# Second layer norm of a fused recurrence and expert block: VectorE reads the two replicated statistics from PSUM, block by block

## The chip, the cores and the metric

One Trainium2 chip, all 8 cores. Each core computes one of the 8 sequences by itself; the cores exchange nothing. The metric is the device time of one execution, in microseconds, of the slowest core. A core has TensorE (PE in the profile), VectorE (DVE), ScalarE (ACT), GpSimd (POOL) and the queues that issue transfers (SP, and GpSimd's own).

## The reference

The input x has 8 sequences of 2048 tokens with 1024 channels, in f32. One layer is computed:

```python
x = x + attn(layernorm(x))      # both layer norms over channels, eps 1e-5
x = x + ffn(layernorm(x))

def attn(x, w_qkva, gamma):     # w_qkva [3072, 1024]
    h = rmsnorm(x) * gamma
    q, kv, a = split(h @ w_qkva.T, 3)
    a = sigmoid(a)
    # y[t] = a[t] * y[t-1] + kv[t], along the tokens
    return q * y

def ffn(x, W1, b1, W2, b2, Wg, bg):          # 8 experts, hidden size 128
    gate = softmax(x @ Wg + bg)
    h = relu(einsum('bsd,edh->bseh', x, W1) + b1)
    y = einsum('bseh,eho->bseo', h, W2) + b2
    return einsum('bse,bseo->bso', gate, y)
```

## The kernel before

Channels lie on the partitions and tokens run along the free dimension: x is handed over transposed and cut into 8 blocks (k, or d) of 128 channels. The 2048 tokens are worked in four chunks (c = 0 to 3) of TC = 512. A tile such as `x2_sb` or `hbf` is 128 x 8 x 512, one block per k. All weights stay in SBUF as bf16.

Per chunk the work goes through these functions, in this order:

- `emitB`: for each of 8 blocks the kv, a and q matmuls (lines 427, 446, 495; eight matmuls each), the sigmoid on ScalarE (458), the scan along the tokens on VectorE (469), the product with q on VectorE (506, into `y_sb`), and the residual addition on GpSimd (518, into `x2_sb` or `x2_sb2`, which the chunks take in turn, the function `x2buf`).
- `emitC`: ScalarE casts x2 to bf16 (533) and squares it (555), TensorE sums both over channels (545, 563), and VectorE and ScalarE make one row of means and one of reciprocal deviations (`emit_rows`, lines 218 to 242).
- `emitY2grp`, `emitOuts`: the previous chunk's second expert matmul, for output blocks d two at a time (853, 856; nine matmuls per block) and the addition into x2 on VectorE (870). It is strewn in between the current chunk's steps.
- `emitLoadXbf`, `emitS1`: the next chunk's x is loaded as bf16 by GpSimd's queue (268) and summed on TensorE (288).
- `emitRep2`: TensorE replicates the two rows over 128 partitions into `ps_rep` (579, 581; reciprocal deviation in bank 0, mean in bank 1), and VectorE copies both to `asig` in SBUF (589, 590).
- `emitLn2` (LN2): hbf = (x2 - mean) * rstd. VectorE does blocks 0 to 4, GpSimd blocks 5 to 7 (628, 631). VectorE takes blocks 0-1 and 2-3 in pairs of 128x1024 (604, 609) and block 4 alone (613, 617). Both engines read the statistics from `asig`.
- `emitScores`: eight matmuls of the gate (654). Block k waits for LN2's block k; in chunks 1 to 3 the first also waits for output addition 2. Then exp (662), its sum (672) and reciprocal (683).
- `emitE1`: the first expert matmul per expert (751), relu (811), replication of the gate into `ps_rep` (769, 801), the product into `h1g` (782, 832), and the next chunk's statistics (GpSimd's square at 315, sums at 331, rows, `emitRep1`). `emitPairs2` forms the next chunk's normed input (394).

The order on each engine is written out by hand; what an engine waits for are counts of one semaphore per engine. Each engine takes its instructions in order. `run_schedule` sets the order around the change. On VectorE it is: copies to `asig`, LN2's blocks, output additions 2, 3, 4, 5 of the previous chunk, the reciprocal of the gate's sum, additions 6 and 7. On TensorE: replication into `ps_rep`, the previous chunk's output groups 2, 3, 4 and 5, the scores, the sum, groups 6 and 7, the h1 matmuls. On GpSimd: residual additions, the issue of the xbf load, LN2's blocks 5 to 7, the square for the next chunk. `ps_rep` is written again by the gate's replication, which waits for VectorE's `g_bf` (705), behind LN2 in VectorE's order.

The copies that stay in both versions:

```python
vector.wait_ge(s_mm.h, K["mm_rep2"])
vector.tensor_copy(asig[:, 0, :], ps_rep[:, 0, :])
ii = vector.tensor_copy(asig[:, 1, :], ps_rep[:, 1, :])
s_dve.inc(ii)
```

Of the kernel before, what the change touches and what calls it, by code (L numbers as in the profile page):

```python
# [7 lines left out]
ALU = mybir.AluOpType  # L8
# [19 lines left out]
def build_program(T=2048, TC=512):  # L28
# [23 lines left out]
    with stack:  # L52
# [20 lines left out]
        hbf = sb("hbf", [128, KC, TC], BF16)  # L73
        y_sb = sb("y_sb", [128, KC, TC], F32)
        x2_sb = sb("x2_sb", [128, KC, TC], F32)
        x2_sb2 = sb("x2_sb2", [128, KC, TC], F32)
        asig = sb("asig", [128, 2, TC], F32)
# [8 lines left out]
        def x2buf(c):  # L86
            return x2_sb if c % 2 == 0 else x2_sb2
# [11 lines left out]
        ps_rep = ps("ps_rep", [128, 2, TC])  # L99
# [10 lines left out]
        s_dve = Sem(stack, nc, "s_dve")  # L110
# [17 lines left out]
        def on(eng, fn):  # L128
            state["on"](eng, fn)
# [5 lines left out]
        def rec_i(lst, i, sem):  # L135
            if state["counting"]:
                lst[i] = sem.n

        def init(d, key):
            if state["counting"]:  # L140
                d[key] = [0] * KC
# [453 lines left out]
        def emitLn2(c):  # L595
            K = ck[c]
            init(K, "ln2k")
            NDVE = 5
            for k0 in (0, 2, 4):
                def _ln2(vector, k0=k0):  # L600
                    if k0 == 0:
                        vector.wait_ge(s_dve.h, K["dve_evac"])
                    if k0 < 4:
                        s_dve.inc(vector.tensor_tensor(  # L604
                            y_sb[:, k0:k0 + 2, :], x2buf(c)[:, k0:k0 + 2, :],
                            asig[:, 1:2, :].to_broadcast([128, 2, TC]),
                            ALU.subtract))
                        vector.wait_ge(s_dve.h, s_dve.n)
                        ii = vector.tensor_tensor(  # L609
                            hbf[:, k0:k0 + 2, :], y_sb[:, k0:k0 + 2, :],  # L610
                            asig[:, 0:1, :].to_broadcast([128, 2, TC]), ALU.mult)
                    else:
                        s_dve.inc(vector.tensor_tensor(y_sb[:, k0, :],
                                                       x2buf(c)[:, k0, :],
                                                       asig[:, 1, :], ALU.subtract))
                        vector.wait_ge(s_dve.h, s_dve.n)
                        ii = vector.tensor_tensor(hbf[:, k0, :], y_sb[:, k0, :],
                                                  asig[:, 0, :], ALU.mult)
                    s_dve.inc(ii)
                on("vector", _ln2)  # L620
                rec_i(K["ln2k"], k0, s_dve)
                if k0 < 4:
                    rec_i(K["ln2k"], k0 + 1, s_dve)
            for k in range(NDVE, KC):
                def _ln2g(gpsimd, k=k):
                    if k == NDVE:
                        gpsimd.wait_ge(s_dve.h, K["dve_evac"])
                    s_gp.inc(gpsimd.tensor_tensor(y_sb[:, k, :], x2buf(c)[:, k, :],  # L628
                                                  asig[:, 1, :], ALU.subtract))
                    gpsimd.wait_ge(s_gp.h, s_gp.n)  # L630
                    ii = gpsimd.tensor_tensor(hbf[:, k, :], y_sb[:, k, :],  # L631
                                              asig[:, 0, :], ALU.mult)
                    s_gp.inc(ii)
                on("gpsimd", _ln2g)
                rec_i(K["ln2k"], k, s_gp)
            if state["counting"]:
                K["dve_ln2"] = K["ln2k"][NDVE - 1]
                K["gp_ln2"] = K["ln2k"][KC - 1]
            K["n_dve_ln2"] = NDVE
# [247 lines left out]
        def run_schedule():  # L887
# [23 lines left out]
            for c in range(NCH):  # L911
# [11 lines left out]
                if c > 0:  # L923
                    emitY2grp(c - 1, [2, 3], c)
                emitLn2(c)
                if c > 0:
                    emitOuts(c - 1, [2, 3])
# [106 lines left out]
```

## Time and profile before

| | us |
|---|---|
| median of 2 runs | 538.6 (538.58 to 538.61) |
| the profiled execution | 538.28 |
| its span on the slowest core (core 3) | 536.7 |
| spans of the 8 cores | 524.1 to 536.7 |
| TensorE busy | 413.1 (77%) |
| VectorE busy | 253.1 (47%) |
| GpSimd busy | 119.2 (22%) |
| ScalarE busy | 114.0 (21%) |

The span runs from the first to the last instruction; the execution's time has 1.6 us around it. The rows are those of core 3 unless they say otherwise. In a timeline a row gives the start, the duration, the engine, the line of the kernel, the operation, output and inputs with partitions x elements and type, and how many instructions were merged (x8); the bracket says how long the engine had been idle before and what released it. PE is TensorE's matmul, DVE VectorE, ACT ScalarE, POOL GpSimd.

### The profile page before, as it was taken

How to read it: one execution, taken by the hardware profiler on the slowest of the kernel's cores; microseconds unless marked ns; L12 is line 12 of the kernel's file. 1: busy time of each engine (PE TensorE's matmuls, PEld its weight loads, DVE VectorE, ACT ScalarE, POOL GpSimd, SP SyncE). 2: the span in 40 equal slices, each digit the busy share in tenths (PEclk: the TensorE clock that was granted, in tenths of full speed). 3: DMA queues.
4: the chain of work that ended last, by engine and by line, in shares of the span. 5: the costliest groups of instructions: out<-in, count | busy, mean ns of one | idle time of the engine just before them, and what ended most of it. 6: DMA issues, size and time to landing. Idle time of an engine off the chain costs nothing.

```text
span 536.7 us, 4715 instructions; the slowest of 8 cores (524.1 to 536.7 us)
## 1 busy us (share of the span) xinstructions
PE 413.1 (77%) x1540; PEld 151.4 (28%) x1540; DVE 253.1 (47%) x319; ACT 114.0 (21%) x179; POOL 119.2 (22%) x76
## 2 busy tenths in 40 slices
PE   1345599713779999767889998687989997858994
PEld 0101144200223444212323443122224442313231
DVE  0463434337465344528365434576554343873221
ACT  2120010720123112510222104500251026102200
POOL 5000012306700013119300024067000212430000
PEclk9955799966597999968978999998879999968888
DMA  7999992280000000720400000900400000004004
GB/s 120 222 169 157 165 166 41 70 167 0 0 0 2 0 1 1 184 52 0 158 0 1 1 0 1 234 2 0 156 1 0 1 0 1 1 0 158 0 0 156
DMA packets 18230, 32.05 MB, mean 60 GB/s; under 512 B 656, under 2 KB 4752, under 8 KB 18208
## 3 DMA queue, kind: packets, MB, share of 16 engines
q0 software_dynamic: 9584, 14.98, 18.0%
q1 hardware_dynamic: 8624, 16.79, 9.5%
q8 instruction: 13, 0.21, 0.2%
q14 instruction: 9, 0.07, 0.0%
HBM read 38.35 MB, written 8.39 MB: 87 GB/s over the span
## 4 chain that ended last, share of the span: by engine, by line
PE 56%; DVE 17%; DMA 16%; issue 4%; ACT 2%; another core or an unknown queue 2%; POOL 1%; DVEq 0%; ACTq 0%; POOLq 0%
PE ps_kv L427 10%; PE ps_a L446 10%; PE ps_q L495 9%; DMA xbf<-xT 9%; DMA wq_bf<-wqT 8%; PE ps_kv L751 7%; PE ps_a L856 4%; DVE hbf L609 3%; PE ps_a L751 3%; DVE y_sb L604 3%; DVE rows L235 2%; PE ps_a L654 2%; PE ps_kv L856 2%; PE ps_q L288 2%
## 5 line engine op out<-in xcount | busy, mean ns | idle before, releaser
L518 POOL TENSOR_TENSOR x_sb<-x_sb,y_sb 128x512 f32<-128x512 f32 x32 | 40.4, 1264 | 274.1 <-DVE y_sb L506 274.0
L427 PE MATMUL ps_kv<-hbf,wq_bf 128*128 128x512 bf16 x256 | 67.3, 397 | 16.4 <-DVE hbf L903 7.5
L446 PE MATMUL ps_a<-hbf,wq_bf 128*128 128x512 bf16 x256 | 62.7, 389 | 6.1 <-DVE wq_bf L199 6.1
L469 DVE TENSOR_TENSOR_SCAN y_sb<-asig,carry,ps_kv 128x512 f32<-128x512 f32 x24 | 30.7, 1280 | 63.5 <-ACT asig L458 63.5
L495 PE MATMUL ps_q<-hbf,wq_bf 128*128 128x512 bf16 x256 | 59.3, 379 | 0.1
L458 ACT ACTIVATE asig<-ps_a 128x512 f32<-128x512 f32 x32 | 19.1, 597 | 158.3 <-PE ps_a L446 158.3
L751 PE MATMUL ps_kv<-hbf,w_bf 128*128 128x512 bf16 x192 | 50.8, 421 | 0.0
L628 POOL TENSOR_TENSOR y_sb<-x_sb,asig 128x512 f32<-128x512 f32 x12 | 25.0, 2082 | 78.7 <-DVE asig L590 78.7
L427 PEld LDWEIGHTS ps_kv<-hbf,wq_bf 128*128 128x128 bf16 x256 | 25.6, 100 | 54.1 <-issue 29.0
L288 PE MATMUL ps_q<-xbf,statc 128*1 128x512 bf16 x32 | 12.4, 550 | 34.2 <-DMA xbf<-xT 34.2
L446 PEld LDWEIGHTS ps_a<-hbf,wq_bf 128*128 128x128 bf16 x256 | 25.5, 100 | 37.9 <-issue 9.5
L495 PEld LDWEIGHTS ps_q<-hbf,wq_bf 128*128 128x128 bf16 x256 | 25.0, 98 | 30.5 <-issue 1.0
L856 PE MATMUL ps_a<-h1g,w_bf 128*128 128x512 bf16 x128 | 33.5, 409 | 0.0
L654 PE MATMUL ps_a<-hbf,wg_bf 128*128 128x512 bf16 x32 | 14.2, 609 | 24.3 <-DVE x_sb L870 13.5
L856 PE MATMUL ps_kv<-h1g,w_bf 128*128 128x512 bf16 x128 | 31.8, 393 | 0.0
L832 DVE TENSOR_TENSOR h1g<-y_sb,ps_rep 128x512 bf16<-128x512 f32 x24 | 16.2, 686 | 29.1 <-ACT y_sb L811 23.1
L751 PEld LDWEIGHTS ps_kv<-hbf,w_bf 128*128 128x128 bf16 x192 | 19.3, 106 | 28.3 <-issue 12.0
L235 DVE RECIPROCAL rows<-rows 1x512 f32<-1x512 f32 x8 | 26.7, 3341 | 0.8
L811 ACT ACTIVATE y_sb<-ps_kv,b1s 128x512 f32<-128x512 f32 x24 | 16.0, 678 | 48.0 <-PE ps_kv L751 48.0
L506 DVE TENSOR_TENSOR y_sb<-ps_q,y_sb 128x512 f32<-128x512 f32 x32 | 22.1, 692 | 7.3 <-PE ps_q L495 6.4
L631 POOL TENSOR_TENSOR hbf<-y_sb,asig 128x512 bf16<-128x512 f32 x12 | 22.6, 1884 | 1.7
L218 DVE COPY rows<-ps_q 1x512 f32<-1x512 f32 x8 | 5.4, 676 | 34.1 <-PE ps_q L288 17.6
(85 smaller groups left out, 430.5 us busy)
## 6 DMA issues: line engine op xcount, KB each, us to landing
x_sb<-xT SPq DMA_DIRECT2D x4, 2048.0 KB, 13.9
outT<-x_sb SPq DMA_DIRECT2D x4, 2048.0 KB, 6.6
wq_bf<-wqT POOLq DMA_DIRECT2D x3, 2048.0 KB, 41.1
xbf<-xT POOLq DMA_DIRECT2D x3, 1024.0 KB, 16.5
w_bf<-w1p POOLq DMA_DIRECT2D x1, 2048.0 KB, 64.5
w_bf<-w2p POOLq DMA_DIRECT2D x1, 2048.0 KB, 76.5
xbf<-xT POOLq DMA_DIRECT2D x2, 512.0 KB, 11.5
wg_bf<-wgp POOLq DMA_DIRECT2D x1, 256.0 KB, 76.0
```

Of the source, the lines that this page charges most:

```text
L235: ii = vector.reciprocal(row(R_INV), row(R_S2))
L288: ii = tensor.matmul(ps_q[0:1, 0, :], statc[:], xbf[:, k, :], start=(k == 0), stop=(k == KC - 1))
L427: ii = tensor.matmul(ps_kv[:, j % 2, :], wq_bf[:, k, (8 + j) * 128:(9 + j) * 128], hbf[:, k, :], start=(k == 0), stop=(k == KC - 1))
L446: ii = tensor.matmul(ps_a[:, j % 2, :], wq_bf[:, k, (16 + j) * 128:(17 + j) * 128], hbf[:, k, :], start=(k == 0), stop=(k == KC - 1))
L469: s_dve.inc(vector.tensor_tensor_scan(y_sb[:, j, :], asig[:, j % 2, :], ps_kv[:, j % 2, :], init, ALU.mult, ALU.add))
L495: ii = tensor.matmul(ps_q[:, j % 2, :], wq_bf[:, k, j * 128:(j + 1) * 128], hbf[:, k, :], start=(k == 0), stop=(k == KC - 1))
L518: ii = gpsimd.tensor_tensor(x2buf(c)[:, j, :], x_sb[:, j, :], y_sb[:, j, :], ALU.add)
L628: s_gp.inc(gpsimd.tensor_tensor(y_sb[:, k, :], x2buf(c)[:, k, :], asig[:, 1, :], ALU.subtract))
L631: ii = gpsimd.tensor_tensor(hbf[:, k, :], y_sb[:, k, :], asig[:, 0, :], ALU.mult)
L654: ii = tensor.matmul(ps_a[:, 0, :], wg_bf[:, k, :], hbf[:, k, :], start=(k == 0), stop=(k == KC - 1))
L751: ii = tensor.matmul(pb[:, BM[e] % 2, :], w1_bf[:, k, e * 128:(e + 1) * 128], hbf[:, k, :], start=(k == 0), stop=(k == KC - 1))
L856: ii = tensor.matmul(pb[:, d % 2, :], w2_bf[:, e, d * 128:(d + 1) * 128], h1g[:, e, :], start=False, stop=(e == E - 1))
```

## The change

In LN2, VectorE's five blocks are taken one at a time in place of two pairs and one, so that ten instructions of 128x512 stand for four of 128x1024 and two of 128x512. Their second operand is the replicated mean or reciprocal deviation in `ps_rep` (PSUM, f32) in place of `asig` (SBUF, f32). VectorE's wait for its own copies to `asig` goes; the wait of each multiplication for its subtraction stays. The copies stay, and GpSimd's blocks 5 to 7 read `asig` as before. Each block has now its own count to wait for (blocks 0 and 1 had one in common, as had 2 and 3).

```diff
--- before.py
+++ after.py
@@ -596,31 +596,16 @@
             K = ck[c]
             init(K, "ln2k")
             NDVE = 5
-            for k0 in (0, 2, 4):
-                def _ln2(vector, k0=k0):
-                    if k0 == 0:
-                        vector.wait_ge(s_dve.h, K["dve_evac"])
-                    if k0 < 4:
-                        s_dve.inc(vector.tensor_tensor(
-                            y_sb[:, k0:k0 + 2, :], x2buf(c)[:, k0:k0 + 2, :],
-                            asig[:, 1:2, :].to_broadcast([128, 2, TC]),
-                            ALU.subtract))
-                        vector.wait_ge(s_dve.h, s_dve.n)
-                        ii = vector.tensor_tensor(
-                            hbf[:, k0:k0 + 2, :], y_sb[:, k0:k0 + 2, :],
-                            asig[:, 0:1, :].to_broadcast([128, 2, TC]), ALU.mult)
-                    else:
-                        s_dve.inc(vector.tensor_tensor(y_sb[:, k0, :],
-                                                       x2buf(c)[:, k0, :],
-                                                       asig[:, 1, :], ALU.subtract))
-                        vector.wait_ge(s_dve.h, s_dve.n)
-                        ii = vector.tensor_tensor(hbf[:, k0, :], y_sb[:, k0, :],
-                                                  asig[:, 0, :], ALU.mult)
+            for k in range(NDVE):
+                def _ln2(vector, k=k):
+                    s_dve.inc(vector.tensor_tensor(y_sb[:, k, :], x2buf(c)[:, k, :],
+                                                   ps_rep[:, 1, :], ALU.subtract))
+                    vector.wait_ge(s_dve.h, s_dve.n)
+                    ii = vector.tensor_tensor(hbf[:, k, :], y_sb[:, k, :],
+                                              ps_rep[:, 0, :], ALU.mult)
                     s_dve.inc(ii)
                 on("vector", _ln2)
-                rec_i(K["ln2k"], k0, s_dve)
-                if k0 < 4:
-                    rec_i(K["ln2k"], k0 + 1, s_dve)
+                rec_i(K["ln2k"], k, s_dve)
             for k in range(NDVE, KC):
                 def _ln2g(gpsimd, k=k):
                     if k == NDVE:
```

## Rows read from the trace of the kernel before

**Rows 1.** Page, the chain that ended last, share of the span by engine

```profile
...
PE 56%; DVE 17%; DMA 16%; issue 4%; ACT 2%; another core or an unknown queue 2%; POOL 1%; DVEq 0%; ACTq 0%; POOLq 0%
...
```

**Rows 2.** The chain in order of time, chunk 0: start us, us, what

```profile
...
135.00 1.57 DVE hbf L617
136.71 1.88 PE ps_a L654 x4
140.08 8.22 PE ps_kv L751 x24
...
```

**Rows 3.** Timeline, VectorE and GpSimd, LN2 of chunk 0: start us, us, engine

```profile
...
125.39 1.23 DVE L604 TENSOR_TENSOR y_sb<-x_sb,asig 128x1024 f32<-128x1024 f32 x1
125.44 2.29 POOL L628 TENSOR_TENSOR y_sb<-x_sb,asig 128x512 f32<-128x512 f32 x1 [22.34 <-DVE asig L590]
126.72 2.10 DVE L609 TENSOR_TENSOR hbf<-y_sb,asig 128x1024 bf16<-128x1024 f32 x1
127.88 2.06 POOL L631 TENSOR_TENSOR hbf<-y_sb,asig 128x512 bf16<-128x512 f32 x1
128.74 2.28 DVE L604 TENSOR_TENSOR y_sb<-x_sb,asig 128x1024 f32<-128x1024 f32 x1
...
135.00 1.56 DVE L617 TENSOR_TENSOR hbf<-y_sb,asig 128x512 bf16<-128x512 f32 x1
136.16 1.53 POOL L631 TENSOR_TENSOR hbf<-y_sb,asig 128x512 bf16<-128x512 f32 x1
...
```

**Rows 4.** Groups by form, whole run: busy us, mean ns

```profile
...
L518 POOL TENSOR_TENSOR x_sb<-x_sb,y_sb 128x512 f32<-128x512 f32 x32 | 40.4, 1264 | 274.1 <-DVE y_sb L506 274.0
...
L832 DVE TENSOR_TENSOR h1g<-y_sb,ps_rep 128x512 bf16<-128x512 f32 x24 | 16.2, 686 | 29.1 <-ACT y_sb L811 23.1 <-PE ps_kv L751 5.7 <-PE ps_rep L801 0.2
...
L222 DVE TENSOR_TENSOR rows<-rows 1x512 f32<-1x512 f32 x8 | 5.4, 671 | 0.0
...
```

**Rows 5.** Timeline, a GpSimd pair beside VectorE with a PSUM input, chunk 0

```profile
...
97.86 2.60 POOL L518 TENSOR_TENSOR x_sb<-x_sb,y_sb 128x512 f32<-128x512 f32 x2 [3.92 <-DVE y_sb L506]
98.36 0.69 DVE L506 TENSOR_TENSOR y_sb<-ps_q,y_sb 128x512 f32<-128x512 f32 x1 [0.64 <-PE ps_q L495]
...
```

**Rows 6.** Timeline, chunk 1: LN2's start, TensorE up to the h1 matmuls

```profile
...
239.90 1.23 DVE L604 TENSOR_TENSOR y_sb<-x_sb,asig 128x1024 f32<-128x1024 f32 x1
...
246.57 1.90 PE L856 MATMUL ps_kv<-h1g,w_bf 128*128 128x512 bf16 x8
...
251.94 3.49 PE L654 MATMUL ps_a<-hbf,wg_bf 128*128 128x512 bf16 x8 [3.46 <-DVE x_sb L870]
...
260.86 5.34 PE L751 MATMUL ps_kv<-hbf,w_bf 128*128 128x512 bf16 x24
...
```

**Rows 7.** Timeline, chunk 2: LN2's start, scores, h1 matmuls

```profile
...
353.12 1.23 DVE L604 TENSOR_TENSOR y_sb<-x_sb,asig 128x1024 f32<-128x1024 f32 x1
...
365.15 3.21 PE L654 MATMUL ps_a<-hbf,wg_bf 128*128 128x512 bf16 x8 [5.04 <-DVE x_sb L870]
...
373.79 5.34 PE L751 MATMUL ps_kv<-hbf,w_bf 128*128 128x512 bf16 x24
...
```

**Rows 8.** Timeline, chunk 3: the same, and the group behind the scores

```profile
...
462.73 1.23 DVE L604 TENSOR_TENSOR y_sb<-x_sb,asig 128x1024 f32<-128x1024 f32 x1
...
474.76 3.57 PE L654 MATMUL ps_a<-hbf,wg_bf 128*128 128x512 bf16 x8 [5.04 <-DVE x_sb L870]
...
480.30 3.59 PE L856 MATMUL ps_a<-h1g,w_bf 128*128 128x512 bf16 x8
...
485.90 5.34 PE L751 MATMUL ps_kv<-hbf,w_bf 128*128 128x512 bf16 x24
...
```

**Rows 9.** Granted clock of chunk 3's scores; core 0's chunk 1, scores and h1

```profile
...
474.76:478.34 3.58, 3.57 (x8) 1.07 (x8) 1.54 (x3) 0.00 (x0) 0.27 (x1) 0.50 0.00 0
...
250.97 1.89 PE L654 MATMUL ps_a<-hbf,wg_bf 128*128 128x512 bf16 x8 [2.37 <-DVE x_sb L870]
...
258.29 4.05 PE L751 MATMUL ps_kv<-hbf,w_bf 128*128 128x512 bf16 x18
...
```

## The prediction

> **What bounds the kernel now.** I read the page's chain of waits by engine first [rows 1]. TensorE's work makes up 56% of the chain that ended last, VectorE's 17%. So most of the time is not where this change works, and the question is in which stretches VectorE or GpSimd decides. The chain in order of time answers it. Its rows here [rows 2] are, for chunk 0, VectorE's last multiplication, the score matmuls and the h1 matmuls; in each of the four chunks the second layer norm (I call it LN2) is on the chain, from the first subtraction to the moment when the score matmuls may run, and it is VectorE's instructions that stand there, one behind the other.
>
> The third view is the timeline of that stretch with VectorE and GpSimd side by side [rows 3]. The first subtraction, 128x1024 f32, takes 1.23 us. The same instruction, issued again at 128.74, takes 2.28. The last multiplication, a single block of 128x512, takes 1.56, more than the first one took for twice the elements. So the length isn't set by the elements. Look at the ends instead: VectorE 126.62, GpSimd 127.73, VectorE 128.82, GpSimd 129.94, VectorE 131.02: they alternate. Each engine finishes about 1.1 us after the other has finished, though both were issued long before. These two engines take turns at something. In these rows all have both inputs in SBUF (x2 and y_sb with asig). The whole stretch is a sum of turns: VectorE runs from 125.39 to 136.56 (11.2 us), GpSimd from 125.44 to 137.69 (12.25 us). The pattern repeats in all four chunks with the same durations.
>
> Does an instruction of VectorE with one input in PSUM take part in this? One place shows it [rows 5]: two GpSimd additions at 97.86 take 2.60 us together, 1.30 each, while VectorE multiplies ps_q by y_sb at 98.36 in 0.69 us. Over the whole run GpSimd's addition takes 1264 ns on average and VectorE's 128x512 multiplication with a PSUM input 686 ns [rows 4]. A turn would have made VectorE's 0.69 longer by up to 1.1 us; it isn't. So a PSUM operand seems to keep VectorE out of the turns.
>
> **The change on VectorE.** Six instructions go (four of 128x1024, two of 128x512); ten of 128x512 come, each with x2 or y_sb in SBUF and ps_rep in PSUM. The nearest rows are the h1g multiplication (SBUF f32 by PSUM f32, bf16 out, 686 ns) [rows 4] and the multiplication by ps_q (f32 out, 0.69) [rows 5]: I take 0.69 each. The multiplication waits for its subtraction: it starts 0.10 us behind the end of that (125.39 + 1.23 = 126.62, start 126.72). The next subtraction waits for nothing and starts 0.08 before the end (126.72 + 2.10 = 128.82, start 128.74) [rows 3]. One block so costs 0.69 + 0.10 + 0.69 - 0.08 = 1.40, five cost 7.0 us, where 11.1 went before: 4.1 us less per chunk. The wait for the copies in front of the first subtraction goes too; since the copies are VectorE's own, the start moves from 0.10 behind them to 0.08 before their end, 0.18 us. The copies to asig themselves stay, since GpSimd reads them.
>
> The Trainium skill has a rule that speaks against this (VectorE: DVE Perf Modes, sections "Rules for kernel authors" and "The TRN2 errata"): for many operations on a matmul's output one copies it to SBUF first, and a PSUM source has a fixed cost of 120 cycles where an SBUF source has 58, at 0.96 GHz. As an estimate by that page the ten would cost 10 x 0.065 = 0.65 us more than from SBUF. In the trace the difference is smaller: 671 ns for a 512-element f32 multiplication out of SBUF beside 686 with PSUM [rows 4], 0.15 us over the ten. The page's price would take 0.65 us from each chunk where VectorE decides, and leave the sign.
>
> **The change on GpSimd**, whose code isn't touched. Its three blocks are two instructions each, 2.29 and 2.06 us, with turns of VectorE in them. Alone, the same shape in f32 takes 1.26 [rows 4]; the part of a turn behind VectorE's end is 1.12 (128.82 to 129.94) [rows 3]. I take 1.26 and keep 1.12 as the low bound, the 2.06 to 2.29 of now as the high one. With 0.15 between subtraction and multiplication: 3 x (1.26 + 0.15 + 1.26) = 8.0 in place of 12.25, 4.25 us less.
>
> **What that is worth, chunk by chunk.** The scores take blocks 0 to 4 from VectorE and 5 to 7 from GpSimd; in chunks 1 to 3 they also wait for output addition 2, queued on VectorE behind LN2, and stand on TensorE behind four groups of the previous chunk's second matmul.
> - Chunk 0 [rows 2, 3]: the last four score matmuls start at 136.71 and are done at 138.58. After: VectorE is through at 132.4, GpSimd at 125.44 + 8.0 = 133.44, and the last matmul ends about 0.8 later (0.14 to wake, 0.6 for one at the low clock), at 134.2. Gain 4.4. GpSimd is what is late now.
> - Chunk 1 [rows 6]: LN2 starts at 239.90, the scores at 251.94. VectorE would let them start at 239.90 + 7.0 + 0.94 = 247.8 (0.94 is from the start of the addition, 11.1 behind LN2's, to the scores), but TensorE has its groups to finish until 246.57 + 1.90 = 248.5. TensorE becomes the limit: gain 3.4.
> - Chunks 2 and 3 [rows 7, 8]: from LN2's start to the scores 12.03 us in both (353.12 to 365.15, 462.73 to 474.76). After: 7.0 + 0.94 - 0.18 = 7.8. Gain 4.25 each, and GpSimd (8.0, with its last block used only after seven matmuls) is in time.
>
> Sum 4.4 + 3.4 + 8.5 = 16.3 us. All of it lies on the chain, and the next chunk's load of xbf, its sums and its first matmuls start from there, so I cost nothing of it away.
>
> **TensorE's clock.** In chunks 1 to 3 TensorE stood still for 3.5 to 5.0 us in front of the scores (the brackets in [rows 6, 7, 8]), and the eight scores took 3.49, 3.21 and 3.57 us; the granted clock of the last of these stretches, the third figure from the end of its row, is 0.50, that is 1.2 GHz [rows 9]. In chunk 3 the group behind them was slow too, 3.59 for what takes 1.90 elsewhere. Core 0, whose pause in chunk 1 was 2.37 us, had the eight at 2.4 GHz in 1.89, and went from the scores to the h1 matmuls in 258.29 - 250.97 = 7.3 us [rows 9]. On core 3 that way took 8.9, 8.6 and 11.1 us [rows 6, 7, 8]. After the change the pause is 0 in chunk 1 and about 0.9 in the others, so I expect 7.3 everywhere: gains of 1.6, 1.3 and 3.8, together 6.7. This is the soft part of the sum. The bounds are 0 and, since any other group of nine may move by 1.7 us either way when the phases shift, some 5 us more.
>
> Forecast: 16.3 + 6.7 = 23.0 us off the profiled execution's 538.3 (its span and 1.6 around it), 515.3; the median of the runs is 0.3 above it: **515.5 us**.
>
> **Rivals.**
> A: the clock gives nothing back; the scores stay at 1.2 GHz because of the waits for exp and for the second statistics around them. Then 16.3 alone: 522.3. For it: in chunk 0 the 24 h1 matmuls behind the scores take 8.22 us [rows 2], in chunk 1 5.34 [rows 6], so the clock can stay low past the scores. Against: core 0.
> B: GpSimd doesn't speed up, its 2.0 to 2.3 us are its own. Then the last block comes 12.3 us behind the start of LN2 as now, and its matmul ends 0.55 later: gains 0.1 and, from the scores' ends of now (255.4, 368.4, 478.3) against 239.9, 353.1 and 462.7 plus 12.85, 2.7, 2.4 and 2.8. Together 8.0: 530.6. Against: 1.26 for the same shape [rows 4], and ends that follow VectorE's.
> C, the one on the slower side: the taking of turns persists, because y_sb and hbf are still written in SBUF and x2 read there. A turn of VectorE for 128x1024 costs 1.08 (129.94 to 131.02 [rows 3]), so one for 128x512 half of that, 0.54, and one of GpSimd 1.12. Six and six alternate, 10.0 us, and four more of VectorE take 2.8: 12.8 in place of 11.1, because more and smaller instructions each wait for a longer one. It is slower than now from a turn of 0.26 us upwards (6 x (0.26 + 1.12) + 2.8 = 11.1). 1.7 us more in each chunk: 545.3. Against: [rows 5]. The Trainium skill (SBUF — State Buffer, section "Who interferes with whom") says that VectorE needs two SBUF inputs for this, reading being what is shared; by that rule C can't happen.
> D: more clock than counted, the shorter pauses keeping further groups fast: three groups of nine at 1.7, 5 us more, 510.5. For it: 3.59 against 1.90 [rows 6, 8]. Against: the pauses behind the h1 matmuls, for the gate, stay as they are.
>
> **How the numbers follow.** Forecast 0.60, A 0.20, D 0.10, B 0.06, C 0.04. The range runs from 509 (D, with GpSimd's turns at their low bound of 1.12 in chunk 0, 0.8 us) to 525 (A with one or two groups of nine at 1.2 GHz more, 1.7 us each). A measurement of this kernel tells about 2% from no change, that is 527.8 and 549.4: forecast, A and D are faster (0.90, less 0.01 for what I haven't thought of), B and C lie within 2% (0.10), and slower by more gets 0.01.
>
> **What would show it.** VectorE's ten LN2 instructions at 0.62 to 0.69 us, whatever GpSimd does beside them; GpSimd's six at 1.26; the scores in chunk 1 directly behind TensorE's group, in 2 and 3 about 7.8 us behind the start of LN2; eight scores in 1.9 us. Instructions of VectorE above 1 us there would mean C; GpSimd still at 2 us, B; scores of 3.5 us, A. The forecast is wrong altogether if the gained time comes back as a longer wait for xbf's load, whose start only moves with the chain.

## The result and the profile after

The changed kernel takes 518.0 us (median), 0.960 of the kernel before (95% interval 0.957 to 0.963): 4.0% less, about 21.7 us of 538.9. The forecast was 515.5 us, with a range of 509 to 525. In some executions, of the kernel before as well, one die runs some per cent longer at a lower granted clock; all ratios leave these out.

The profiled execution took 516.0 us (538.3 before) and has a span of 514.4 us on core 7, where the one before had 536.7 on core 3. The mean span of the eight cores fell from 531.4 to 509.0. The chain that ended last, share of the span by engine, from the page:

```profile
...
PE 61%; DMA 17%; DVE 12%; issue 3%; ACT 2%; another core or an unknown queue 2%; POOL 1%; DVEq 0%; ACTq 0%; POOLq 0%
...
```

VectorE's share of the chain has gone from 17% to 12% [rows 1]. The timeline of LN2 in chunk 0, VectorE, GpSimd and TensorE (start us, us, engine, line; LN2's lines are now 601 and 604 on VectorE, 613 and 616 on GpSimd, the scores 639, the h1 matmuls 736):

```profile
...
126.04 0.68 DVE L601 TENSOR_TENSOR y_sb<-x_sb,ps_rep 128x512 f32<-128x512 f32 x1
126.28 1.26 POOL L613 TENSOR_TENSOR y_sb<-x_sb,asig 128x512 f32<-128x512 f32 x1 [22.38 <-DVE asig L590]
126.82 0.69 DVE L604 TENSOR_TENSOR hbf<-y_sb,ps_rep 128x512 bf16<-128x512 f32 x1
127.43 0.68 DVE L601 TENSOR_TENSOR y_sb<-x_sb,ps_rep 128x512 f32<-128x512 f32 x1
...
127.68 1.27 POOL L616 TENSOR_TENSOR hbf<-y_sb,asig 128x512 bf16<-128x512 f32 x1
...
132.96 1.26 POOL L616 TENSOR_TENSOR hbf<-y_sb,asig 128x512 bf16<-128x512 f32 x1
...
133.21 1.86 PE L639 MATMUL ps_a<-hbf,wg_bf 128*128 128x512 bf16 x4 [0.80 <-DVE hbf L604]
...
136.50 0.13 PEld L736 LDWEIGHTS ps_kv<-hbf,w_bf 128*128 128x128 bf16 x2 [0.47 <-issue]
...
```

Set this beside [rows 3]. VectorE's and GpSimd's instructions lie across each other and neither is longer for it: 0.68 and 0.69 beside 1.26 and 1.27. No end of the one follows the end of the other any more. VectorE starts at 126.04 and is through after 7.0 us, where it took 11.2; GpSimd ends at 134.22, 7.9 us after its start, where it took 12.25. The groups by form over the whole run say the same (busy us, mean ns):

```profile
...
L616 POOL TENSOR_TENSOR hbf<-y_sb,asig 128x512 bf16<-128x512 f32 x12 | 15.2, 1268 | 1.7
L613 POOL TENSOR_TENSOR y_sb<-x_sb,asig 128x512 f32<-128x512 f32 x12 | 15.2, 1268 | 82.1 <-DVE asig L590 82.1
...
L604 DVE TENSOR_TENSOR hbf<-y_sb,ps_rep 128x512 bf16<-128x512 f32 x20 | 13.7, 687 | 2.1
L601 DVE TENSOR_TENSOR y_sb<-x_sb,ps_rep 128x512 f32<-128x512 f32 x20 | 13.6, 679 | 0.0
...
```

Chunk 1, VectorE's first subtraction, TensorE's last group of the previous chunk, the output additions, the scores, the h1 matmuls. It answers to [rows 6]:

```profile
...
234.14 0.68 DVE L601 TENSOR_TENSOR y_sb<-x_sb,ps_rep 128x512 f32<-128x512 f32 x1
...
240.97 1.90 PE L841 MATMUL ps_kv<-h1g,w_bf 128*128 128x512 bf16 x8
...
241.09 1.28 DVE L855 TENSOR_TENSOR x_sb<-ps_a,x_sb 128x512 f32<-128x512 f32 x2
...
242.70 1.89 PE L639 MATMUL ps_a<-hbf,wg_bf 128*128 128x512 bf16 x8
...
250.02 5.34 PE L736 MATMUL ps_kv<-hbf,w_bf 128*128 128x512 bf16 x24
...
```

The row of the scores has no bracket: TensorE came from its group, which ends at 242.87, without a pause (matmuls are pipelined, so a row can start before the end of the one in front). VectorE would have let them start at 242.03 (output addition 2 starts at 241.09, and before it was 0.94 from there to the scores). So TensorE is what decides here, as the prediction had it. Chunk 2 is alike, which the prediction did not have: behind a late replication the first of the previous chunk's groups (L841) runs at the low clock.

```profile
...
343.60 3.59 PE L841 MATMUL ps_a<-h1g,w_bf 128*128 128x512 bf16 x8
...
344.55 0.68 DVE L601 TENSOR_TENSOR y_sb<-x_sb,ps_rep 128x512 f32<-128x512 f32 x1
...
354.12 1.89 PE L639 MATMUL ps_a<-hbf,wg_bf 128*128 128x512 bf16 x8
...
```

Chunk 3, beside [rows 8]:

```profile
...
449.88 0.68 DVE L601 TENSOR_TENSOR y_sb<-x_sb,ps_rep 128x512 f32<-128x512 f32 x1
...
457.75 1.89 PE L639 MATMUL ps_a<-hbf,wg_bf 128*128 128x512 bf16 x8 [0.69 <-DVE x_sb L855]
...
465.07 5.34 PE L736 MATMUL ps_kv<-hbf,w_bf 128*128 128x512 bf16 x24
...
```

From LN2's start to the scores 7.87 us (12.03 before), from the scores to the h1 matmuls 7.32 (11.14). The granted clock of these scores, the third figure from the end:

```profile
...
457.75:459.65 1.90, 1.89 (x8) 0.74 (x8) 1.54 (x3) 0.00 (x0) 0.32 (x1) 1.00 0.00 0
...
```

It was 0.50 in [rows 9]. The same two stretches, read from the timelines of all eight cores for chunks 1 to 3 (24 stretches a kernel):

| | LN2's start to scores, mean | pause before the scores | eight scores in 1.89 us | scores to h1 matmuls, mean |
|---|---|---|---|---|
| before | 12.04 | 2.1 to 5.0 | 7 of 24 | 9.47 |
| after | 8.58 (7.9 where VectorE decides) | 0 to 0.7 | 24 of 24 | 7.32 |

So per core the mean gain in three chunks is 3 x (12.04 - 8.58) = 10.4 us of position and 3 x (9.47 - 7.32) = 6.5 us of clock.

### The profile page after: what moved, and what is told of

It reads as the page before. It is cut to its first block, busy times and chain, and to the rows that moved or that the text cites. A ratio compares the mean times of both kernels' runs of the same rounds, so it can differ in the third digit from the quotient of the medians.

```text
span 514.4 us, 4735 instructions; the slowest of 8 cores (503.4 to 514.4 us)
## 1 busy us (share of the span) xinstructions
PE 405.8 (79%) x1540; PEld 149.8 (29%) x1540; DVE 235.3 (46%) x335; ACT 114.0 (22%) x179; POOL 102.0 (20%) x76
## 4 chain that ended last, share of the span: by engine, by line
PE 61%; DMA 17%; DVE 12%; issue 3%; ACT 2%; another core or an unknown queue 2%; POOL 1%; DVEq 0%; ACTq 0%; POOLq 0%
PE ps_kv L427 11%; PE ps_a L446 10%; PE ps_q L495 10%; DMA xbf<-xT 9%; DMA wq_bf<-wqT 8%; PE ps_kv L736 7%; PE ps_a L841 6%; PE ps_kv L841 3%; PE ps_a L736 3%; DVE rows L235 3%; PE ps_q L288 2%; PE ps_a L639 1%; DVE wq_bf L199 1%; DVE hbf L604 1%
## 5 line engine op out<-in xcount | busy, mean ns | idle before, releaser
L458 ACT ACTIVATE asig<-ps_a 128x512 f32<-128x512 f32 x32 | 19.1, 597 | 159.5 <-PE ps_a L446 159.5
L736 PE MATMUL ps_kv<-hbf,w_bf 128*128 128x512 bf16 x192 | 48.7, 407 | 0.0
L288 PE MATMUL ps_q<-xbf,statc 128*1 128x512 bf16 x32 | 13.9, 605 | 35.4 <-DMA xbf<-xT 35.4
L841 PE MATMUL ps_a<-h1g,w_bf 128*128 128x512 bf16 x128 | 33.8, 412 | 0.0
L841 PE MATMUL ps_kv<-h1g,w_bf 128*128 128x512 bf16 x128 | 31.8, 393 | 0.0
L613 POOL TENSOR_TENSOR y_sb<-x_sb,asig 128x512 f32<-128x512 f32 x12 | 15.2, 1268 | 82.1 <-DVE asig L590 82.1
L817 DVE TENSOR_TENSOR h1g<-y_sb,ps_rep 128x512 bf16<-128x512 f32 x24 | 16.2, 685 | 26.5 <-ACT y_sb L796 21.7
L315 POOL TENSOR_TENSOR tbf<-xbf 128x4096 bf16<-128x4096 bf16 x3 | 21.0, 7012 | 0.0
L211 ACT ACT_TABLE_LOAD x16 | 20.5, 1283 | 1.5 <-ACT y_sb L796 0.4
```

The lines of the kernel that those rows point to most:

```text
L211: ii = scalar.activation(plscr[:], plscr[:], func)
L288: ii = tensor.matmul(ps_q[0:1, 0, :], statc[:], xbf[:, k, :], start=(k == 0), stop=(k == KC - 1))
L315: ii = gpsimd.tensor_tensor(xsq[:], xbf[:], xbf[:], ALU.mult)
L736: ii = tensor.matmul(pb[:, BM[e] % 2, :], w1_bf[:, k, e * 128:(e + 1) * 128], hbf[:, k, :], start=(k == 0), stop=(k == KC - 1))
L841: ii = tensor.matmul(pb[:, d % 2, :], w2_bf[:, e, d * 128:(d + 1) * 128], h1g[:, e, :], start=False, stop=(e == E - 1))
```

## The experiments

Each kernel was timed beside the kernel before on the same chip; ratios are against that one.

**e1: small blocks, operands in SBUF.** The changed kernel, with asig for ps_rep:

```diff
+                    if k == 0:
+                        vector.wait_ge(s_dve.h, K["dve_evac"])
                     s_dve.inc(vector.tensor_tensor(y_sb[:, k, :], x2buf(c)[:, k, :],
-                                                   ps_rep[:, 1, :], ALU.subtract))
+                                                   asig[:, 1, :], ALU.subtract))
                     vector.wait_ge(s_dve.h, s_dve.n)
                     ii = vector.tensor_tensor(hbf[:, k, :], y_sb[:, k, :],
-                                              ps_rep[:, 0, :], ALU.mult)
+                                              asig[:, 0, :], ALU.mult)
```

> The ten small instructions of the changed kernel, but with both statistics read from asig in SBUF (and the wait for the copies kept). Theory (VectorE and GpSimd take turns while both instructions read two operands from SBUF; the operand's place made the gain): the turns persist, VectorE's LN2 takes 12.8 us per chunk where it took 11.1, the time is about 545 us, 1.2% above the kernel before. Rival R1 (a PSUM operand is quicker for VectorE by itself, GpSimd has no part): about as before, 539. Rival R2 (small blocks with counts of their own made the gain): as the changed kernel, 517.

568.4 us, ratio 1.054 (1.050 to 1.057). R2 has fallen: the small blocks alone make the kernel slower. It is slower than the theory said, too, by 23 us. Its timeline in chunk 0, a multiplication of VectorE (L606), the last of GpSimd's LN2 (L618), and GpSimd's square for the next chunk (L315):

```profile
...
134.61 1.56 DVE L606 TENSOR_TENSOR hbf<-y_sb,asig 128x512 bf16<-128x512 f32 x1
135.77 1.53 POOL L618 TENSOR_TENSOR hbf<-y_sb,asig 128x512 bf16<-128x512 f32 x1
...
137.26 7.46 POOL L315 TENSOR_TENSOR tbf<-xbf 128x4096 bf16<-128x4096 bf16 x1
137.95 7.31 DVE L606 TENSOR_TENSOR hbf<-y_sb,asig 128x512 bf16<-128x512 f32 x1
...
```

GpSimd has only six instructions in LN2, VectorE ten. When GpSimd has finished its six it doesn't fall silent: its queue holds the square of 128x4096, 7 us. Here the turn lasts as long as that whole instruction. VectorE's multiplication, issued at 137.95, ends at 145.26, 0.54 us after the square. From LN2's start to the scores it is therefore 20.4 us in chunks 1 and 2, and 13.8 in chunk 3, which has no square behind it. Chunk 1:

```profile
...
249.73 0.69 DVE L603 TENSOR_TENSOR y_sb<-x_sb,asig 128x512 f32<-128x512 f32 x1
...
270.12 3.57 PE L641 MATMUL ps_a<-hbf,wg_bf 128*128 128x512 bf16 x8 [11.69 <-DVE x_sb L857]
...
```

**e9: e1 with the square held back.**

```diff
                 gpsimd.wait_ge(s_mm.h, ck[c - 1]["mm_s2b"])
+                gpsimd.wait_ge(s_dve.h, ck[c - 1]["dve_ln2"])
                 ii = gpsimd.tensor_tensor(xsq[:], xbf[:], xbf[:], ALU.mult)
```

> e1 (ten small instructions from asig) with one wait more: GpSimd's square for the next chunk starts only when VectorE's LN2 is through. In e1's trace VectorE's fourth multiplication waits 7.3 us behind that square in chunks 0 to 2. If that one turn is what put e1 at 568 where rival C was priced at 545, LN2 to scores takes 13.8 us in all of chunks 1 to 3, as it did in e1's chunk 3, which has no square, and the time falls by 3 x 4.3 = 13 to some 20 us (with a shorter pause for TensorE's clock), to 545 to 555 us. If the small blocks had a cost of their own in SBUF, it stays above 560.

547.9 us, ratio 1.016 (1.006 to 1.027): inside what I had expected, and slower than the kernel before by 0.6 to 2.7%. Chunk 1 of its trace, GpSimd's last LN2 instruction (L619), VectorE's multiplications beside and behind it (L607), the square (L316) and the scores (L642):

```profile
...
250.42 1.57 DVE L607 TENSOR_TENSOR hbf<-y_sb,asig 128x512 bf16<-128x512 f32 x1
251.58 1.53 POOL L619 TENSOR_TENSOR hbf<-y_sb,asig 128x512 bf16<-128x512 f32 x1
...
253.75 0.69 DVE L607 TENSOR_TENSOR hbf<-y_sb,asig 128x512 bf16<-128x512 f32 x1
...
255.99 7.01 POOL L316 TENSOR_TENSOR tbf<-xbf 128x4096 bf16<-128x4096 bf16 x1 [2.89 <-DVE hbf L607]
...
256.70 3.57 PE L642 MATMUL ps_a<-hbf,wg_bf 128*128 128x512 bf16 x8 [5.07 <-DVE x_sb L858]
...
```

From 253.11 on GpSimd is silent, and the same VectorE instruction that took 1.57 beside it takes 0.69. LN2 to the scores is 13.8 us in all three chunks (256.70 - 242.93), on all cores. The one wait is worth 20 us: an added wait that makes a kernel faster. It saves 6.6 us in each of the three chunks with a square behind them: 20.4 to 13.8 in chunks 1 and 2, and 24.4 to 17.7 from the copies to the h1 matmuls in chunk 0, which my expectation had left out. What is left over the kernel before is the price of small turns against long ones, 13.8 against 12.0 us: on the mean of the cores 7.3 us from the copies to the h1 matmuls, of the 1.6% or 8.8 us.

**e2: pairs, operands in PSUM.** The kernel before, its two pairs kept:

```diff
                         s_dve.inc(vector.tensor_tensor(
                             y_sb[:, k0:k0 + 2, :], x2buf(c)[:, k0:k0 + 2, :],
-                            asig[:, 1:2, :].to_broadcast([128, 2, TC]),
+                            ps_rep[:, 1:2, :].to_broadcast([128, 2, TC]),
                             ALU.subtract))
```

and the same in the other three places, and without the wait for the copies.

> The kernel before with its two pairs and one single block, only the operand moved from asig to ps_rep. Theory: VectorE's pairs take 1.23 us each and LN2 2 x 2.48 + 1.40 = 6.4 us (7.0 in the changed kernel); GpSimd's six at 1.27. TensorE or GpSimd hides most of the 0.6 in chunks 0 to 2: 516.5 to 517.5 us. R1: the same. R2: no gain, 538.

514.6 us, ratio 0.956 (0.953 to 0.959), 1.9 us below the range that I had given. Timeline, chunk 0, pair subtraction and pair multiplication of VectorE, GpSimd between them:

```profile
...
125.92 1.21 DVE L602 TENSOR_TENSOR y_sb<-x_sb,ps_rep 128x1024 f32<-128x1024 f32 x1
126.16 1.26 POOL L626 TENSOR_TENSOR y_sb<-x_sb,asig 128x512 f32<-128x512 f32 x1 [23.80 <-DVE asig L590]
127.24 1.22 DVE L607 TENSOR_TENSOR hbf<-y_sb,ps_rep 128x1024 bf16<-128x1024 f32 x1
...
```

1.21 and 1.22 us for 1024 elements, where [rows 3] has 2.10 for the same multiplication. So the operand's place gives the whole gain (with the wait for the copies, 0.18 us a chunk, which goes along with it), and the split into single blocks none. The median is even 3.4 us below the changed kernel's, which was timed apart from it, but the intervals overlap (up to 0.959 here, from 0.957 there), so whether pairs are better isn't settled. The traces have LN2 to the scores at 7.24 us where VectorE decides, against 7.87.

**e5: all eight blocks on VectorE, operands in SBUF, GpSimd idle.** The kernel before with

```diff
-            NDVE = 5
-            for k0 in (0, 2, 4):
+            NDVE = 8
+            for k0 in (0, 2, 4, 6):
```

all of them pairs from asig, and the square held as in e9. The sigmoid, which writes into `asig`, waits for VectorE's last block in place of GpSimd's.

> The kernel before, with all eight LN2 blocks on VectorE in four pairs from asig, and GpSimd's square for the next chunk held until they are done, so that GpSimd is idle. Theory (turns): every instruction of 128x1024 takes 1.23 us although both operands lie in SBUF, LN2 takes 4 x 2.48 = 9.9 us for eight blocks where five took 11.1 with GpSimd's help. Scores 1.2 us earlier in chunks 1 to 3, 2.1 in chunk 0, and perhaps some of the clock: 530 to 534 us, faster than the kernel before with half the engines at work. R1 (VectorE is slow from SBUF by itself): 8 x 2.1 = 16.8 us, 5.7 later in each chunk, 561 us.

531.7 us, ratio 0.988 (0.983 to 0.993): a small gain, as expected and clear of the noise. Timeline, chunk 0, the first pair:

```profile
...
127.07 1.23 DVE L605 TENSOR_TENSOR y_sb<-x_sb,asig 128x1024 f32<-128x1024 f32 x1
128.40 1.23 DVE L610 TENSOR_TENSOR hbf<-y_sb,asig 128x1024 bf16<-128x1024 f32 x1
...
```

1.23 us each, and all of them, in every chunk and on every core, are 1.22 or 1.23. R1 has fallen: SBUF operands (1.23) are as quick as PSUM operands (1.22 in e2) as long as GpSimd is silent. In the kernel before, GpSimd's help was worth less than nothing: VectorE does eight blocks alone in 10.0 us and needed 11.2 for five with it.

**e3: only the subtractions read PSUM.**

```diff
                     ii = vector.tensor_tensor(hbf[:, k, :], y_sb[:, k, :],
-                                              ps_rep[:, 0, :], ALU.mult)
+                                              asig[:, 0, :], ALU.mult)
```

> As the changed kernel, but the multiplications read the reciprocal deviation from asig; the subtractions keep ps_rep. Theory: subtractions at 0.68 us beside GpSimd, multiplications at 0.69 to 1.8 (their own 0.54 and what is left of GpSimd's 1.12), VectorE's LN2 about 10 us, GpSimd's about 10.5 to 11: 530 to 536 us. R1: each PSUM operand is worth the same, half of the gain, 528, with all multiplications equally long. R2: 517.

524.8 us, ratio 0.976 (0.972 to 0.981): between, but better than I expected. Timeline, chunk 0, a subtraction of GpSimd (L613) with VectorE's subtraction from PSUM (L601) and multiplication from SBUF (L604) beside it:

```profile
...
129.03 1.71 POOL L613 TENSOR_TENSOR y_sb<-x_sb,asig 128x512 f32<-128x512 f32 x1
129.54 0.67 DVE L601 TENSOR_TENSOR y_sb<-x_sb,ps_rep 128x512 f32<-128x512 f32 x1
...
130.32 0.97 DVE L604 TENSOR_TENSOR hbf<-y_sb,asig 128x512 bf16<-128x512 f32 x1
...
```

VectorE's subtraction runs through at 0.67 inside GpSimd's turn; the multiplication issued behind it waits for what is left of that turn (it ends 0.55 behind GpSimd's end at 130.74) and takes 0.97. I had not counted that the free subtraction eats up most of the turn that the multiplication would otherwise wait for: VectorE's LN2 takes 8.75 us and not 10. R1 doesn't fit here either: the first multiplication of each chunk takes 1.27 and the four others 0.97, the same operands each time. LN2 to the scores is 9.6 us. The turns belong to the single instruction and its operands, not to the stage.

**e4: the pause given back.** The changed kernel with work for nothing behind VectorE's LN2 in chunks 1 to 3:

```diff
+            if c > 0:
+                def _fill(vector):
+                    vector.wait_ge(s_dve.h, s_dve.n)
+                    s_dve.inc(vector.tensor_copy(row(R_T0), row(R_S2)))
+                    vector.wait_ge(s_dve.h, s_dve.n)
+                    s_dve.inc(vector.reciprocal(row(R_GI), row(R_T0)))
+                on("vector", _fill)
```

> The changed kernel with work that isn't needed behind VectorE's LN2 in chunks 1 to 3: a copy and a reciprocal of one row of 512, some 3.9 us, in front of output addition 2. It gives TensorE back its pause before the scores and leaves both LN2 halves free of turns. By position alone: the filler less the slack that the additions have in the changed kernel's profile (0.7 in chunk 1, 1.7 in chunk 2, none in chunk 3), 3.2 + 2.2 + 3.9 = 9.3 us, 527 us. If the pause also costs TensorE its clock in the scores and the group behind, as in the kernel before, up to 6.7 us more: 533 us, eight scores at 3.5 us instead of 1.9.

537.3 us, ratio 0.998 (0.996 to 0.999): the gain is gone, and 4 us more than expected with it. Some 3 of these 4 us are position: the filler is 4.7 us long (241.99 in chunk 1 to 246.69, where the next addition starts), not 3.9. Timeline, chunk 1, GpSimd's last LN2 instruction (L623), the copy (L612), the reciprocal (L614):

```profile
...
241.78 1.27 POOL L623 TENSOR_TENSOR hbf<-y_sb,asig 128x512 bf16<-128x512 f32 x1
...
241.99 1.34 DVE L612 COPY rows<-rows 1x512 f32<-1x512 f32 x1
...
243.43 3.34 DVE L614 RECIPROCAL rows<-rows 1x512 f32<-1x512 f32 x1
...
```

The copy has one input, in SBUF, and takes 1.34 us; a one-row operation of 512 elements, the cast in line 221, takes 0.42 when GpSimd is still (a copy of such a row with GpSimd still is in no trace). All 24 copies stand beside GpSimd's last instruction and take 1.33 to 1.35. The one shown ends 0.28 us behind GpSimd's instruction (243.05). So one SBUF input is enough for a copy to take its turn, which I hadn't expected from [rows 5]. The Trainium skill says it (SBUF — State Buffer, section "Who interferes with whom"): a copy can run in a mode that uses both ports and then contends, whereas a `tensor_tensor` contends by its second SBUF input. As to who waits the trace agrees, with 1.34 for the copy, and with 0.68 beside GpSimd for a `tensor_tensor` with one SBUF input.

LN2's start to the scores is 12.7 us, 4.1 more than after the change on average over the 24 stretches, 12.4 us in three chunks where I had 9.3. The clock comes back as I had priced it. The scores to the h1 matmuls are back at a mean of 9.55 us where the changed kernel has 7.32 everywhere: 6.7 us in three chunks. Together 19.1 of the some 20 us between the two kernels by their ratios (0.998 and 0.960). Granted clock in chunk 3, scores and the group behind them (the third figure from the end):

```profile
...
473.82:477.40 3.58, 3.57 (x8) 1.07 (x8) 1.54 (x3) 0.00 (x0) 0.00 (x0) 0.50 0.00 0
479.36:482.90 3.54, 3.54 (x10) 1.08 (x9) 2.99 (x1) 0.00 (x0) 0.00 (x0) 0.53 0.00 0
...
```

Nothing about these matmuls was changed; what is new is that TensorE had stood still for 5.52 us in front of them. Of the 24 stretches, those with a pause of 2.5 to 2.9 us had the scores in 1.89, and every one above 3.8 had at least some of them at the low clock. The length of the pause doesn't decide alone, though. In the chunks 1 to 3 of all eleven traces together, the scores took 1.89 us behind every pause up to 1.3 us and behind none above 3.4; of the 30 pauses between 2.1 and 3.0 us, 19 left them at 1.89 and 11 did not (9 of these in e3, 2.33 to 2.77 us behind pauses of 2.42).

**e6, e7, e8: where the gained time would come back.** The prediction named a longer wait for xbf's load as what would undo it. The load is issued from GpSimd's queue behind the residual additions, though its buffer is free before `emitB` begins. Moved there in the changed kernel (e6), in the kernel before (e7), in e2 (e8):

```diff
             for c in range(NCH):
+                if c + 1 < NCH:
+                    emitLoadXbf(c + 1)
                 emitB(c)
...
                 if c + 1 < NCH:
-                    emitLoadXbf(c + 1)
                     emitS1(c + 1)
```

> The changed kernel with the next chunk's load of xbf issued ahead of emitB in place of behind it. TensorE's waits for that load (10.2, 5.6 and some 2.6 us in the changed kernel's trace) should go; the replication then waits for the row of deviations, 14.6 us behind the last product with q as in chunk 3, in place of 22.5, 22.3 and 17.9, plus up to 3 us for the sums of xbf in front: 10 to 16 us less, 501 to 507 us. Rival: the load collides with the weights' and with x_sb's and comes no earlier in chunk 0: 5 to 8 us less.

489.9 us, ratio 0.910 (0.904 to 0.916), 11 us below the range that I had given.

> The kernel before with the same earlier load. If LN2's gain and the load's are independent stretches of the chain, the two differ by as much as the kernels with the late load (4%): 523 to 529 us. If the change's gain depended on the load's wait in any way, the distance to e6 is smaller than 21 us.

521.3 us, ratio 0.968 (0.962 to 0.973), 2 us below my range.

> Pairs from PSUM and the earlier load: VectorE's LN2 6.4 us in place of 7.0; since TensorE binds in chunks 1 and 2, 0 to 1 us below e6.

490.6 us in the profiled execution, ratio 0.912 (0.906 to 0.918), e6's within the intervals. My reason, that TensorE hides what the pairs save, doesn't hold: LN2 to the scores is 7.5 us on average where e6 has 7.9, and TensorE itself is late in 3 of the 24 stretches only. The mean span of the cores is all the same 486.3 against 486.2. Where the saved half microsecond a chunk goes is not shown.

The waits for that load on the slowest core of the changed kernel (us in total, times, longest):

```profile
...
PE ps_q L288 <- DMA xbf<-xT: 35.4, 5, 10.4
...
```

and in e6:

```profile
...
PE ps_q L288 <- DMA xbf<-xT: 15.4, 2, 10.4
...
```

20 us of it are gone; what is left are the two halves of the first chunk's load, at the start. The sums of xbf (L288) in front of chunk 1's LN2, in the changed kernel (core 7):

```profile
...
226.83 3.57 PE L288 MATMUL ps_q<-xbf,statc 128*1 128x512 bf16 x8 [5.61 <-DMA xbf<-xT]
...
```

The same sums in e6, with the replication (L579), LN2's start and the scores:

```profile
...
212.48 1.89 PE L288 MATMUL ps_q<-xbf,statc 128*1 128x512 bf16 x8
...
214.30 1.12 PE L579 MATMUL ps_rep<-rows,ones_f 1*128 1x512 f32 x2
...
216.94 0.68 DVE L601 TENSOR_TENSOR y_sb<-x_sb,ps_rep 128x512 f32<-128x512 f32 x1
...
224.83 1.89 PE L639 MATMUL ps_a<-hbf,wg_bf 128*128 128x512 bf16 x8 [0.70 <-DVE x_sb L855]
...
```

The sums now run at a granted clock of 1.00 in 1.89 us directly before the replication, where they took 3.57 at 0.50 behind a wait, and LN2 starts at 216.9 in place of 234.1. I had e6 at 501 to 507 and was wrong by more than 10. From the start to the first LN2, and from each LN2 to the next, it gains 8.3, 8.9, 7.9 and 1.5 us (126.0 to 117.7; 108.1 to 99.2; 110.4 to 102.6; 105.3 to 103.9). From the start of the last product with q to the replication, core 7 of the changed kernel has 22.5, 22.3 and 20.0 us in chunks 0 to 2, and e6 has 14.5, 14.9 and 14.9, sums and all: 20.5 us. I had 17.9 for the third, which isn't core 7's, and added up to 3 us for the sums, which cost next to nothing. Another 2.2 us are scores that no longer stand behind TensorE in chunks 1 and 2. Where the last 4 lie wasn't worked out. The cores now end within 4.8 us of each other (483.1 to 487.9), where they spread over 11.0 (503.4 to 514.4).

The distance between e7 and e6 is 31.4 us, where the late load had 21.7. I had put down a smaller distance as the sign that the gain depends on the load's wait; it does depend, and the distance is larger. In e7 the pause before the scores is 5.0 to 5.2 us on all cores in chunks 1 and 2, and the way from the scores to the h1 matmuls has a mean of 10.9 us; in e6 the pause is 0.7 to 0.9 and the way 7.3. Position 3 x 4.15, the earlier start 3 x 0.19 and clock 3 x 3.54, with chunk 0's 4.3, are 28.0 of the 31.4; with the late load the same steps give 21.8. Of the 6 us between, 2 are position: with the early load TensorE no longer reaches the replication late and at the low clock, and VectorE decides in all 24 stretches of e6. The other 4 are clock: the pause of e7 costs more than that of the kernel before (on average 4.7 us long against 3.8, and 10.9 us from the scores to the h1 matmuls against 9.5), so there is more to give back.

## Why the prediction was right

By its own steps, on the slowest core of each profile:

| step | forecast | measured |
|---|---|---|
| VectorE's LN2 | 7.0 us, 0.69 each | 7.0, 0.68 and 0.69 |
| start against the copies | 0.18 earlier | 0.19 (125.45 + 0.68 - 126.04 = 0.09 before their end, 0.10 behind it before) |
| GpSimd's LN2 | 8.0 us, 1.26 each | 7.9, 1.27 |
| chunk 0, copies to h1 matmuls | 4.4 less | 4.4 (16.0 to 11.7) |
| chunk 1: position, clock | 3.4, 1.6 | 3.7, 1.6 |
| chunk 2: position, clock | 4.25, 1.3 | 2.65, 1.3 |
| chunk 3: position, clock | 4.25, 3.8 | 4.35, 3.8 |

Position is the way from LN2's start to the scores, with the 0.19 of the earlier start; clock is the way from there to the h1 matmuls. The sum comes to 21.8 us where I had 23.0. By its span the profiled execution gained 22.3 us. The difference between 23.0 and 21.8 has one place: in chunk 2 of core 7 TensorE reached the replication behind a late load, ran the previous chunk's first group at the low clock (3.59 us) and was not through with its four groups when VectorE was; VectorE took 7.0 us but the scores started after 9.57. I had read that limit in chunk 1 of core 3 and taken chunk 2 as VectorE's. On the eight cores, TensorE decides in 11 of the 24 stretches.

The table sets core 3 of one trace against core 7 of another, and how well single lines agree is in part luck. From LN2 to LN2 and on to the end, core 7 is shorter than core 3 by 6.4, 2.8, 4.3 and 9.5 us, where the steps say 4.4, 5.3, 4.0 and 8.2; the ways between the stages moved by up to 2.5 us either way and cancelled. The firmer ground is the mean of all eight cores: the same steps give 4.3 + 10.4 + 0.6 + 6.5 = 21.8 us, and the spans 22.3. So almost nothing came back elsewhere, as the prediction had assumed; the waits for xbf's load in front of the three later chunks are 18.0 us a core before and 17.8 after. The profiled execution is 0.7 us above its forecast of 515.3. The median is 2.5 us above the forecast of 515.5, since the profiled execution is one of the quicker ones: those that the ratio counts run from 514.4 to 522.0, a spread wider than the step from the forecast to rival A.

The core of the argument was that VectorE and GpSimd take turns, and that a PSUM operand frees VectorE. Both are shown: the first by e5 (GpSimd silent, SBUF operands, 1.23 us) and e9 (the same instruction at 1.57 and then 0.69), the second by e2 and e3. In e3 the two kinds stand one behind the other. That it is the reading of the second operand, and not the writing, rests on these kernels writing the same tiles in SBUF with and without turns.

The clock was the soft part and the 6.7 us were right, by the means of 24 stretches (6.5) and by e4 (6.7 back). Rival A (no clock) would have been 522.3. The time alone, 518.0, lies between it and the forecast and doesn't exclude it; the 24 scores of 1.89 us do. D asked for 5 us more and didn't come: the previous chunk's groups of eight matmuls lose 4.8 us to the low clock on core 7, where core 3 lost 4.4 before.

Rival B fell with GpSimd's 1.27. Rival C did not occur, and e9 is the kernel in which it does: I had priced it at 545.3 us and 1.7 us a chunk; measured are 547.9 us and 1.74 a chunk (13.78 - 12.04). But that price held only with the square held back. Where the turns really persisted (e1), the price was 568. The step that failed there is "four more of VectorE take 2.8": I asked what VectorE does when GpSimd has finished its share of LN2, and not what GpSimd does next. For the chance of C it made no difference; had C come, it would have been outside my range and slower by more than 2%, not within it. The price of a PSUM operand did not show: subtraction and multiplication take 679 and 687 ns with it here, 685 and 693 ns from SBUF beside a silent GpSimd in e9. (The 671 ns that I had set beside the 686 were of an instruction on one partition.) By the Trainium skill (VectorE: DVE Perf Modes, section "The TRN2 errata", 120 cycles against 58) it would have been, as an estimate, 0.65 us a chunk; the measurement decides.

## What to carry to other kernels

When two engines' instructions end one behind the other at a fixed distance although both were issued long before, they take turns, and the first question is which operand puts them there; moving one operand to PSUM freed both engines here. Price such a turn by the longest instruction that can stand in the other engine's queue, also the one behind the stage, and check whether dividing or delaying the work is better before adding help. Where a stage in front of TensorE gets shorter, add what the pause cost TensorE's clock, which here was two fifths of the gain from position, and look for the next late thing: here a load issued behind work that it doesn't need, worth some 27 us more by the ratios.

## What I had not expected

- A turn is one whole instruction of the other engine: 7.31 us for a multiplication of 0.69, behind a square of 7 us (e1).
- A copy with a single SBUF input takes its turn as well, 1.34 us for one row of 512 (e4), though a `tensor_tensor` with one input in SBUF and one in PSUM doesn't.
- One added wait for GpSimd made a kernel 20 us faster (e1 to e9).
- The gain of the change was larger with an earlier load (31.4 us) than without (21.7).
